# Three step-table edits in a two-layer attention and mixture-of-experts kernel: earlier row loads for the odd parts, a shorter tail for the third batch, a later return of the third batch

## The reference

```python
x = x + tanh(g_xattn[0]) * L0_xattn(layernorm(x), ctx)      # rotary q and k, softmax, Wo, bo
x = x + tanh(g_ffn[0])   * L0_ffn(layernorm(x))             # top 1: relu(x W1 + b1) W2 + b2, times its probability
x = x + tanh(g_xattn[1]) * L1_xattn(layernorm(x), ctx, mask)# masked softmax
x = x + tanh(g_ffn[1])   * L1_ffn(layernorm(x))             # top 2: (silu(x Wg) * (x Wu)) Wd, softmax of the two
```

## Time and profile before

| what | value |
|---|---|
| runs, median (lowest to highest) of 3 | 458.64 us (451.64 to 460.27) |
| the profiled execution, its own time | 455.05 us |
| its span, first to last instruction | 453.3 us |
| mean granted clock of the matmul engine | 0.855 |
| matmul engine (PE) busy | 339.5 us, 75% |
| VectorE (DVE) / ScalarE (ACT) / GpSimd (POOL) busy | 253.6 / 156.5 / 149.8 us |
| DMA | 70.42 MB, mean 155 GB/s |

### The profile page before, as it was taken

One profiled execution on the slowest core, in us unless ns is written; L12 is line 12 of the kernel. 1 busy time (PEld: TensorE's weight loads), 2 busy tenths in 40 slices (PEclk: granted clock), 3 DMA queues, 4 the chain that ended last, 5 costly groups with the idle time before them and its releaser, 6 DMA issues. The chain is left out here.

```text
span 453.3 us, 6857 instructions
## 1 busy us (share of the span) xinstructions
PE 339.5 (75%) x2066; PEld 249.3 (55%) x2066; DVE 253.6 (56%) x846; ACT 156.5 (35%) x370; POOL 149.8 (33%) x172
## 2 busy tenths in 40 slices
PE   2468979888969776466887999997577719988870
PEld 2236545545435665465664575653277609878770
DVE  2759565666365566136747677865463604535542
ACT  2312344434322253124222455362221305444440
POOL 3211211215040340431062102274536565645560
PEclk9867699998695899569869999999787867999995
DMA  7436987940044283776440231013565366869934
GB/s 268 128 75 158 300 230 220 290 133 17 2 148 136 78 246 101 242 219 164 106 129 6 62 80 48 14 35 91 196 199 168 119 172 191 284 187 324 371 139 139
DMA packets 67908, 70.42 MB, mean 155 GB/s; under 512 B 7933, under 2 KB 50691, under 8 KB 67872
## 3 DMA queue, kind: packets, MB, share of 16 engines
q1 hardware_dynamic: 41904, 52.24, 39.6%
q10 hardware_dynamic: 22448, 11.41, 8.7%
q0 software_dynamic: 3520, 6.34, 4.3%
HBM read 40.66 MB, written 21.81 MB: 138 GB/s over the span
## 5 line engine op out<-in xcount | busy, mean ns | idle before, releaser
L963 PE MATMUL ps_s<-xT,fw 128*128 128x128 f32 x488 | 77.7, 303 | 17.0 <-DVE xT L1301 8.6
L963 PEld LDWEIGHTS ps_s<-xT,fw 128*128 128x128 f32 x488 | 69.4, 215 | 20.1 <-DVE xT L1301 10.4
L668 ACT ACTIVATE probs<-ps_s 103x512 f32<-103x512 f32 (+1 forms) x96 | 56.2, 596 | 65.4 <-PE ps_s L872 57.8
L1152 DVE TENSOR_REDUCE negm<-ps_a 128x4 f32<-128x308 f32 x128 | 55.1, 470 | 29.5 <-PE ps_a L852 23.1
L574 POOL DMA_INDIRECT routed<-pay,slot x48 | 48.0, 1001 | 57.1 <-DVE slot L1261 45.9
L592 POOL DMA_INDIRECT expert_out<-xt x46 | 45.8, 996 | 35.1 <-ACT xt L733 25.2
L852 PE MATMUL ps_a<-ks,qs 128*128 128x308 f32 x128 | 42.3, 366 | 10.4 <-DVE negm L1152 5.5
L1291 DVE SCALAR_TENSOR_TENSOR qr<-qr,ps_s 128x256 f32<-128x256 f32 x46 | 19.2, 418 | 53.9 <-ACT qr L723 32.6
L871 PE MATMUL ps_s<-qs,ks 128*103 128x512 f32 (+1 forms) x96 | 47.7, 496 | 1.9 <-issue 0.7
L548 POOL TENSOR_SCALAR ve<-mv 128x4 f32<-128x4 f32 x16 | 3.7, 230 | 121.1 <-DVE mv L1102 121.1
L872 PE MATMUL ps_s<-augT,aug 128*103 128x512 f32 (+1 forms) x96 | 40.3, 420 | 0.0
(11 more groups left out here) (156 smaller groups left out, 559.6 us busy)
## 6 DMA issues: line engine op xcount, KB each, us to landing
fw<-f_in SPq DMA_DIRECT2D x46, 384.0 KB
routed<-xt ACTq DMA_DIRECT2D x2, 5568.0 KB, 23.8
fw<-f_in SPq DMA_DIRECT2D x30, 321.0 KB
qs<-qhl SPq DMA_DIRECT2D x128, 64.0 KB, 2.0
xt<-routed SPq DMA_DIRECT2D x46, 65.0 KB
xt<-routed SPq DMA_DIRECT2D x30, 64.0 KB
routed<-xt SPq DMA_DIRECT2D x30, 64.0 KB
routed<-pad SPq DMA_DIRECT2D x18, 65.0 KB, 2.1
```

Source lines behind the costliest of these rows:

```text
L668: nc.scalar.activation(probs[0:KSIZE[j], s, :], ps_s[(NS * n + s) % SCORE_BANKS][0:KSIZE[j], :], ACT.Exp, scale=SCALE).then_inc(exp_ok, 1)
L963: last = nc.tensor.matmul(up_bank[j % 2][:, c * P:(c + 1) * P], weights_of(j)[:, c * P:(c + 1) * P], xT[j % 2][:, :], start=True, stop=True)
L1152: nc.vector.tensor_reduce(negm[:, i, g * HPG:(g + 1) * HPG], a[:, 0:GK].rearrange("p (h k) -> p h k", h=HPG), AX.X, ALU.max, negate=True). ...
```

## The change

A second table, `TAIL_NEXT_TO_LAST`, gives the third batch of both layers its own tail steps: normalise2 at 20 (was 23), turn2 21 (23), router 22 (25), route_exp 23 (26), ranks 24 (28), scatters 25, 25, 26, 26 (29, 31, 34, 35). So for n = 2 normalise2 and turn2 go from step 47 to 44 and 45, router from 49 to 46, ranks from 52 to 48; for n = 6 normalise2 and turn2 go from 142 to 139 and 140, router from 144 to 141, ranks from 147 to 143. The third batch's return into layer 1 moves from steps 99 to 103 to steps 101 to 104. The first rows of parts 1 and 3 are loaded at steps 65 and 167 instead of 69 and 171.

```diff
+TAIL_NEXT_TO_LAST = {
+    "stats2": 19, "normalise2": 20, "turn2": 21, "router": 22, "route_exp": 23, "ranks": 24,
+    "scatter0": 25, "scatter1": 25, "scatter2": 26, "scatter3": 26,
+}
 TAIL = {
...
-    {"gather": 90, "results": 99, "stats": 99, "normalise": 100, "turn": 101, "project": 102, "high": 103, "low": 103},
+    {"gather": 90, "results": 101, "stats": 101, "normalise": 102, "turn": 103, "project": 104, "high": 104, "low": 104},
...
-    return SECOND * l + NS * b + (TAIL[stage] if b == NB - 1 and stage in TAIL else AT[stage])
+    tail = {NB - 1: TAIL, NB - 2: TAIL_NEXT_TO_LAST}.get(b, {})
+    return SECOND * l + NS * b + tail.get(stage, AT[stage])
...
-                        if k == TILE_AT[p] + max(-1, t - ROWS_AHEAD):
+                        if k == TILE_AT[p] + max(-5 if p % 2 else -1, t - ROWS_AHEAD):
                             load_rows(p, t)
```

## The result

| | before | after |
|---|---|---|
| median of the runs taken together, us | 455.82 (451.64 to 460.27, 4 runs) | 463.1 (461.44 to 464.93, 4 runs) |
| ratio of the times | 1 | 1.0239, 95% interval 1.0168 to 1.031 |
| profiled execution, us | 455.05 (span 453.3) | 464.93 (span 463.1) |
| mean granted clock | 0.855 | 0.857 |

What follows compares the result with a forecast made beforehand. It took waits between engines, and so the order of PE's queue, to bound the kernel. +3.0 + 4.5 - 1.9 + 1.5 - 4.0 - 1.2 = +1.9 us, 460.5 on the median of 458.64; 8 in 10 range 449 to 470.

Steps and rivals of the forecast that it cites:

- Part A, layer 0: Third batch's tail, layer 0: PE waits longer at turn2 with ready work behind it, +3.0 us (0 to +7.2).
- Part A, layer 1: Third batch's tail, layer 1: work behind turn2 +3.0, ranks +3.1, slack -1.6, so +4.5 us (0 to +7.7).
- The rule of the Trainium skill: At lengthened PE waits: following matmuls run on the slow clock, paid at every wait; parts A and B cost upper bounds.
- The unnamed pieces: Chain pieces of 3.75, 7.23 and 5.95 us, from 347.48 to 374.05; half the first counted back, -1.9 us.
- The sign to look for that I had named: Part 2, first to sixteenth tile: a change over 5 us means the unnamed pieces decide and the sum says little.
- Part B: Third batch's return into layer 1: PE waits 4.1 us at the later turn, +1.5 us (-2.6 to +3).
- Part C, part 1: Early rows at part 1: first tile 5.3 us sooner, partly paid back on SP's queue, -4.0 us (-5.3 to 0).
- Part C, part 3: Early rows at part 3: the 1.19 us wait for rows goes, -1.2 us (-1.2 to 0).
- the first, the slower side: Steps 45 and 140: longer turn2 waits put PE on the lower clock level, +12.7 us, 471.3 us; chance 0.15.
- the second: Faster: the unnamed pieces go with the scatters, all 16.9 us gained, -13.1 us, 445.5 us; chance 0.15.

Runs made afterwards that it cites:

- e5: The kernel before with the third batch's new tail table in layer 0 alone; ratio 1.0152 (0.9987 to 1.0317).
- e1: The kernel before with the third batch's new tail table in both layers, nothing else changed; ratio 1.0094 (1.0050 to 1.0137).
- e6: The kernel before with the third batch's new tail table in layer 1 alone; ratio 1.0036 (0.9963 to 1.0109).
- e4: The kernel before with only router, its exponential, ranks and scatters of the third batch sooner in both layers, turn2 and statistics unmoved; ratio 0.9947 (0.9905 to 0.9989).
- e2: The kernel before with only the third batch's return moved later, to steps 101 to 104; ratio 1.0162 (1.0067 to 1.0257).
- e3: The kernel before with only the early row loads at parts 1 and 3; ratio 1.0021 (0.9967 to 1.0074).
- e11: As e4 but in layer 1 alone, the last two pairs of scatters at 31, behind the last batch's root; ratio to the kernel before 0.9859, median 445.98 us.
- e12: e11 with the last batch's scatters of layer 1 spread in pairs at 23, 25, 27 and 29; ratio to the kernel before 0.9907 (0.9870 to 0.9944).

## Why the prediction was right and where it was wrong

The number was right, the way to it only in part: the waits at turn2, at `ranks` and at the return came nearly as forecast, while the prices of the work behind them, of the return and of the scatters did not.

- **Part A, layer 0** (+3.0, bounds 0 and 7.2): measured +4.0 between the two profiles, +4.7 and +4.8 in e5 and e1. The wait of 6.7 came as 6.61. The term that was too small is the work that now stands behind it: "That is +3.0 us at full clock" took 4.9 us, since `weigh1` ran at the lower level. The clock did come back sooner behind it, as forecast: the key spread takes 1.64 us instead of 2.52. (The prediction's two figures for the lower level, 5.6 and 3.6 + 2.3, don't agree with each other; the bounds use the second.)
- **Part A, layer 1** (+4.5, bounds 0 and 7.7): measured +7.4, in e1 and e6 +8.2 and +8.1, at the upper bound or just past it. The wait (5 to 6) came as 5.53, `ranks` (3) as 2.71. Again the term that was too small is `weigh1` and the two score tiles, 3.0 forecast and 5.2 measured. The rule of the Trainium skill, TensorE: Matmul & The Clock Gate, section "HAM oscillation — how this bites in real kernels", which put parts A and B at their upper bounds, was the better guide for this term: 1.94 and 1.93 us a group instead of 1.07. In layer 0 the cost stayed well under the upper bound, because what followed ran faster than before, and the miss in part B is not the clock's (13.93 us behind the turn at the same 0.88 as before).
- **The unnamed pieces** (-1.9, bounds 0 and 16.9): -6.5 in *part 2*, and -7.0 and -7.1 in e6 and e1. The step that failed is "I can't tie them to the scatters; I count half of the first". The length of the stretch hangs on the scatters: e4 has the gain without turn2 moved, and e5, which leaves the scatters of n = 6 in place, doesn't. The sign to look for that I had named, over 5 us in that stretch, came.
- **Part B** (+1.5, bounds -2.6 and +3): +5.3 in e2, +7.3 us timed, and +7.0 between the two profiles, of which 1.8 lie ahead of the edit. This is the largest miss, and past its bound. The 4.1 us wait was near (4.82). Two steps failed. DVE was to start behind "the units of step 101, which come at about 243", 2.9 us later than before; it starts 5.5 us later in the kernel after and 6.3 in e2, and stands 2.20 us for these units, which PE reaches only behind a `weigh` group. And I charged only the difference of the waits and took PE's work ahead of it as won back ("PE, no longer held at step 101, goes through two more score tiles"); at most 0.3 us of it came off behind the turn. DVE's start alone gives the cost.
- **Part C, part 1** (-4.0, bounds -5.3 and 0): first tile -5.0 (5.3 predicted), but +3.1 behind it, net -1.9 by the turn of n = 4, and timed alone nothing. The failed step is "DVE needs its rows only seven steps on": the gather, 4.9 us later, did hold DVE (4.73 us) and, as the tile work stands behind it on DVE, PE (5.02).
- **Part C, part 3** (-1.2): the step that failed is that the wait of 1.19 us was the rows' to give back. It is 0.46 us in the kernel after, but also 0.46 to 0.69 in nine of the kernels that load these rows as before. And *rest* is 3.4 us longer. Whether the edit has a share in that is open: it is 0.4 us above the longest *rest* without it, e2's 60.53, and e3, which has it, stands at 59.28.
- **The sum.** Term by term between the two profiles, measured less forecast: tails +1.0 and +2.9, unnamed pieces -4.6, part B +5.5, part C +2.1 at part 1, *rest* +4.6, together +11.5; with the forecast +1.9 this is +13.4, and *start*, 3.6 us shorter by chance, makes it the +9.8 of the spans. The forecast time came close because it was put on top of a median, 458.6, that was a high draw. Of the rivals the first, the slower side, had the right mechanism for the tails (14.9 priced, 11.4 measured), and the second was right that the pieces go with the scatters, though 7 us and not 16.9 were to be had; none had DVE's later start.

What stays open: what the pieces in *part 2* are. POOL's records there stand 1.27 us apart, and the chain's pieces are times in which ACT waits though PE's matmuls are shown done; e4, e6 and e11 show that the number of the scatters matters and e12 that their spacing does, not through which resource. That the gather holds part 1 through DVE rests on the timelines; a kernel with the gather earlier and the rows early was not run.

## What to carry to other kernels

Price a moved step by when its slow producer starts and by what the consumer engine does behind the wait, clock included, not by the difference of two waits. Don't pull a waiting instruction ahead of ready work to bring its consumers forward: e11 moved only the consumers and kept 3.8 of the 7 us without the price. An early load on an in-order DMA queue is paid by what it overtakes; find who waits for the last of those. Measure how much a stretch varies where nothing was edited before a difference in it is given to the edit: *returns* and *rest* vary by 4 to 5 us here, *middle* by 0.07.

## What the runs showed of the hardware

Two things I had not expected. Eight indirect DMAs on POOL's queue, whose rows are wanted only much later, lengthen the tiles beside them by 6 to 7 us.

In the same place SP needs long for the eight pad stores of its plan. The kernel after at the plan of part 2 and at that of part 3:

```profile
314.97 3.84 SPq L445 DMA_DIRECT2D routed<-pad  x8
...
364.05 9.03 SPq L445 DMA_DIRECT2D routed<-pad  x8
```

The first take 3.84 us in every profile, 0.48 each; the second take 6.8 to 9.0 us, 0.85 to 1.13 each. This does not go with the scatters of n = 6: before, with them, it is 7.11 us, and in e4, without them, 9.02. What it goes with was not tried.

The granted clock of *rest* differs from one profile to the next, 0.94 to 1.00, without an edit that would account for it; why was not tried. Only e12's 0.92, with 64.29 us, lies outside of that, and there the longer *rest* (+7.8 us on e11) was more than the gain of 4.9.
